# Two vision layers on one core: one stream of window pairs over all strips, queries in two buffers made a strip ahead, keys and values loaded in halves, one chain of square roots a strip

## What is computed

```
# layer 0: window attention with a halo, then a small network
x = x + proj(softmax(q k^T + relative position) v)   # 8x8 windows, 6 heads of 16,
                                                     # keys and values from the 12x12 around each window
x = x + quantised_mlp(layernorm(x))                  # 96 -> 384 -> 96, fp8 products
# layer 1: clustering, then a small network
f, v = conv1x1(norm(x))                              # folded into 4 quadrants, 4 heads
sim  = sigmoid(beta + alpha * cos(centres, f)); one centre wins for each point
x = x + proj(sum of the won centres' values)
x = x + quantised_mlp(layernorm(x))
```

## Time and profile before

| | us |
|---|---|
| median of 3 runs | 8823.7 (8789.32 to 8832.83) |
| the profiled execution, its own time | 8806.34 |
| its span, first to last instruction | 8804.6 |
| TensorE matmul busy | 6983.3 |
| TensorE weight loads busy (beside the matmuls) | 5559.6 |
| VectorE busy | 6471.8 |
| ScalarE busy | 4502.9 |
| GpSimd busy | 2616.0 |
| mean granted TensorE clock | 0.865 of 2.4 GHz |

### The profile page before, as it was taken

How to read it: one execution, slowest core, us unless ns; L and a number is a source line. 1 busy time by engine, 2 the same in 40 slices (tenths; PEclk the granted TensorE clock), 3 DMA queues, 4 the chain that set the end, 5 groups by cost and what they waited for, 6 DMA issues and landing times.

```text
span 8804.6 us, 408965 instructions
## 1 busy us (share of the span) xinstructions
PE 6983.3 (79%) x161908; PEld 5559.6 (63%) x161908; DVE 6471.8 (74%) x23705; ACT 4502.9 (51%) x8986; POOL 2616.0 (30%) x4382
## 2 busy tenths in 40 slices
PE   5888888877888888888888878888788878886555
PEld 4666666766666666666666666666666666664332
DVE  3666667667787778777787877777777878786566
ACT  2444444444555555555555555555555555554455
POOL 2333333232333232322323232322323233332112
PEclk7888888888998889888898988989898989898765
DMA  3333333333343433333333333434333333332211
GB/s 82 70 69 69 70 67 71 69 78 76 82 86 81 85 76 82 85 82 81 79 88 80 86 79 80 84 83 85 77 82 80 84 82 83 83 83 65 66 55 53
DMA packets 819501, 681.29 MB, mean 77 GB/s; under 512 B 656745, under 2 KB 690345, under 8 KB 817695
## 3 DMA queue, kind: packets, MB, share of 16 engines
q1 hardware_dynamic: 817918, 657.52, 34.0%
HBM read 350.43 MB, written 227.25 MB: 66 GB/s over the span
## 4 chain that ended last, share of the span: by engine, by line
PE 61%; DVE 15%; issue 13%; ACT 9%; DMA 1%; ACTq 1%; SPq 0%; POOL 0%; DVEq 0%; POOLq 0%
PE scores_x L718 11%; PE bank L695 8%; PE flipped L742 6%; DVE maxes L1562 4%; PE bank L698 4%; PE pv L769 3%; PE bank L678 3%; DVE shifted L1570 3%; PE bank L962 2%; PE bank L662 2%; PE flipped L989 2%; PE pv L763 2%; PE misc L796 2%; PE bank L671 2%; ACT probs L1239 2%
## 5 line engine op out<-in xcount | busy, mean ns | idle before, releaser
L1992 POOL TENSOR_SCALAR x_new<-x_new,mv_x,rs_x 120x96 f32<-120x96 f32 x1170 | 844.5, 734 | 4281.4 <-DVE rs_x L1468 4281.4
L1562 DVE TENSOR_REDUCE maxes<-scores_x 128x6 f32<-128x864 f32 x1024 | 1078.1, 1053 | 837.3 <-PE scores_x L718 831.0
L718 PE MATMUL scores_x<-keys,queries 64*64 64x144 f32 x24576 | 1114.8, 316 | 361.7 <-DVE shifted L1570 274.9
L698 PE MATMUL bank<-xr,wq 97*32 97x64 f32 x24576 | 1071.0, 253 | 216.1 <-issue 215.6
L695 PE MATMUL bank<-xt,wq 97*32 97x64 f32 x24576 | 1065.2, 253 | 222.5 <-issue 210.2
L718 PEld LDWEIGHTS scores_x<-keys,queries 64*64 64x64 f32 x24576 | 818.2, 146 | 560.8 <-issue 523.7
L695 PEld LDWEIGHTS bank<-xt,wq 97*32 97x32 f32 x24576 | 935.2, 132 | 339.9 <-issue 251.8
L698 PEld LDWEIGHTS bank<-xr,wq 97*32 97x32 f32 x24576 | 934.9, 132 | 262.6 <-issue 262.0
L1570 DVE TENSOR_TENSOR shifted<-scores_x,maxes 128x768 f32<-128x768 f32 x1024 | 970.4, 948 | 0.0
L1202 ACT ACTIVATE queries<-bank 128x512 f32<-128x512 f32 x768 | 456.0, 594 | 963.8 <-PE bank L698 961.2
L742 PE MATMUL flipped<-ident,shifted 128*128 128x128 f32 x6144 | 914.2, 288 | 0.6 <-ACT probs L1236 0.4
(11 more groups left out here) (194 smaller groups left out, 14423.0 us busy)
## 6 DMA issues: line engine op xcount, KB each, us to landing
vmain<-v_kept SPq DMA_DIRECT2D x384, 204.0 KB, 4.7
keys<-kst SPq DMA_DIRECT2D x768, 101.2 KB
v_kept<-v_new SPq DMA_DIRECT2D x128, 430.3 KB
x_new<-x_dram SPq DMA_DIRECT2D x130, 409.2 KB, 3.9
xn_kept<-xn SPq DMA_DIRECT2D x128, 388.0 KB, 3.7
later<-xn_kept SPq DMA_DIRECT2D x128, 388.0 KB, 3.3
x_tok<-tok_dram SPq DMA_DIRECT2D x128, 384.0 KB, 3.4
x_kept<-x SPq DMA_DIRECT2D x128, 384.0 KB, 4.4
```

What stands on the lines that cost most here:

```text
L698: last = mm(dst[64 * e + 32:64 * e + 64, :, j, :], wq[0:PROW, 2 * WS + j, 2 * g + e, :], xr[0:PROW, p, j, :, :], start=True, stop=True, sk ...
L718: last = mm(score[e][64 * j:64 * j + 64, g * NKEY:(g + 1) * NKEY], queries[64 * e:64 * e + 64, g, w, :], keys[64 * e:64 * e + 64, g, :, WS ...
L1562: V.tensor_reduce(maxes[:, p % 2, :, :], sc, AX.X, ALU.max).then_inc(max_ready.sem, 1)
L1992: last = P.tensor_scalar(x_new[:, t, 0:C], x_new[:, t, 0:C], mv_x[:, t, 0:1], rs_x[0:XP, t:t + 1], ALU.subtract, ALU.mult)
```

## The change

- **One stream of pairs.** The tail is gone. In pair 7 of strip `n`, TensorE makes the scores of pair 0 of strip `n + 1`; the last `weigh` of a strip stands in pair 0 of the next one. The filler work of all stages is dealt out anew over the eight pairs of all engines: a function of strip `n` is now often called one strip later (`flip_heads(n - 1, 1)`, `mix(n - 1, ...)`, `output(n - 2, ...)`).
- **Queries a strip ahead.** `queries` has two buffers. The six groups of strip `n + 1` are made in pairs 2, 4, 5 and 6 of strip `n`. `x1` has two buffers too.
- **Loads in halves.** Keys are loaded in 2 x 6 transfers and values in 2 x 11. The first half waits for the middle of the strip before, the second for its end.
- **One chain of roots a strip.** `all_roots` in pair 4 makes the roots for x, the stream, both halves of the network, stage c and the feature lengths in one chain of 65 columns.
- The input strip is loaded three strips ahead instead of two. The queue of SyncE has another order.

```
-        queries = sb("queries", [128, NG, NW, 64])
+        queries = sb("queries", [128, 2, NG, NW, 64])
...
+            def load_values(m, column, h):
+                if h == 0:
+                    sp.wait_ge(v_saved, m * 16 + V_TOPS + 16)
+                        sp.wait_ge(pv_ready.sem, pv_ready.at(m - 1, 4))
+                else:
+                    sp.wait_ge(pv_ready.sem, pv_ready.at(m, 0))
...
+            def load_keys(n, h):
+                if h == 0:
+                    sp.wait_ge(k_stored.sem, k_stored.at(n, 3))
+                    sp.wait_ge(halo_k.sem, halo_k.at(n, 1))
+                        sp.wait_ge(s_ready.sem, s_ready.at(n - 1, 4))
+                else:
+                    sp.wait_ge(s_ready.sem, s_ready.at(n, 0))
...
# TensorE
+            def strip(n, par, on, edge_=None):
+                for p in range(TILES):
+                    if p + 1 < TILES:
+                        scores(n, p + 1, par)
+                    elif ahead:
+                        scores(n + 1, 0, 1 - par)
+                    if p == 3 and on.b:
+                        features(n, 0)
...
+                    flip(n, p, 0, on)
+                    flip(n, p, 1, on)
+                    if p > 0:
+                        weigh(n, p - 1, on.bp)
+                    else:
+                            gather(n - 1, 1 - par)
+                            pool(n - 3)
+                            weigh(n - 1, TILES - 1)
+                    if p == 0:
+                            output(n - 2, 0)
+                            output(n - 2, 1)
+                            for u in range(2):
+                                pe.wait_ge(mixed.sem, mixed.at(n - 1, u + 1))
+                                flip_zc(n, u)
+                            make_keys(n + 1, 0, on)
+                            make_keys(n + 1, 1, on)
+                    if p in (1, 2) and on.c3:
+                        hidden_c(n, 2 * p - 2)
+                        hidden_c(n, 2 * p - 1)
+                    if p == 1:
+                            make_keys(n + 1, 2)
+                            make_values(n + 1, 0)
+                            make_values(n + 1, 1)
+                            flip_heads(n - 1, 1)
+                            edge(edge_[0], n, edge_[1], edge_[2], on)
+                    if p == 2:
+                            project(n - 1, 1)
+                            make_queries(n + 1, 0, on)
+                            make_queries(n + 1, 1, on)
+                    if p == 3:
+                            features(n, 1)
+                            hidden_c(n, 4)
+                            hidden_c(n, 5)
+                            flip_features(n + 1, 0, 1 - par)
+                    if p == 4:
+                            make_queries(n + 1, 2, on)
+                            flip_features(n + 1, 1, 1 - par)
+                            output_c(n, 0)
+                            output_c(n, 1)
+                            flip_sims(n)
+                    if p == 5:
+                            make_queries(n + 1, 3, on)
+                            hidden(n - 1, 0)
+                            hidden(n - 1, 1)
+                        flip_heads(n, 0, b1)
+                            make_queries(n + 1, 4, on)
...
# VectorE, behind the subtraction of pair p
+                    if p == 0:
+                            hidden(n - 2, 4)
+                            hidden(n - 2, 5)
+                            mix(n - 1, 0, 1 - par, work)
+                            mix(n - 1, 1, 1 - par, work)
+                            stats_c(n, 1 - par)
+                    if p == 1:
+                            normalise(n - 1, 1, slot if on.b3 else None, n - 3, n - 1 if on.bp else None)
+                            edge(edge_[0], n, edge_[1], edge_[2])
+                            output(n - 2, par)
+                            next_stats(n - 2)
...
+                    if p == 3:
+                            residual(n - 1, 1, 1 - par)
+                            ffn_stats(n - 1, 1, 1 - par)
+                            compare(n, 0)
+                            compare(n, 1)
+                            squares_sum(n, 0)
+                            squares_sum(n, 1)
+                    if p == 4:
+                        all_roots(n, 0, ROOTS, ...)
+                            cosine(n, n)
+                            ffn_apply(n - 1, 0, 1 - par, n)
+                    if p == 5:
+                        normalise(n, 0)
+                            ffn_apply(n - 1, 1, 1 - par, n)
+                            best_of(n, 0)
```

More of the change, by code:

```diff
@@ L605, in _ @@
                 first = max((j - 1) * COLUMN, LAG_C + 2)
-                with sp.Fori(0, (j * COLUMN - 2 - first) // 2) as s:
+                last = j * COLUMN - 2 if j < STARTS else N - 4
+                with sp.Fori(0, (last - first) // 2) as s:
                     for par in range(2):
@@ new lines, in project @@
+            def project(n, b, again=True):
+                pe.wait_ge(heads_t_ready.sem, heads_t_ready.at(n, b + 1))
+                if b == 0 and again:
+                    pe.wait_ge(zt_ready.sem, zt_ready.at(n - 1, 2))
+                pe.sem_inc(gate, 1)
+                for j in range(4):
+                    last = mm(misc[:, j * C:(j + 1) * C], heads_t[0:PROW, j * 128:(j + 1) * 128],
+                              wp[0:PROW, :], start=True, stop=True)
+                last.then_inc(proj_ready.sem, 1)
@@ L1140, in _ @@
                     n = STRIPS * r + 2 + k
-                    if n < N:
-                        strip(n, k, stage(n))
-                    else:
-                        drain(n, k, stage(n))
+                    drain(n, k, stage(n))
             for n in range(N + LAG_C, N + LAG_C + 2):
@@ L1402, in drain, with strips @@
                     for i in range(2 * NK):
-                        hidden_c(n, i)
+                        hidden_c(n + 1, i)
                         if i >= 1:
-                            quantise_c(n, i - 1)
-                    quantise_c(n, 2 * NK - 1)
+                            quantise_c(n + 1, i - 1)
+                    quantise_c(n + 1, 2 * NK - 1)
+            def strips(first, last, on):
+                with act.Fori(0, (last - first) // 2) as s:
+                    for par in range(2):
+                        strip(2 * s + (first + par), on, par)
             setup()
```

1407 lines of the change are left out of this document (710 added, 697 removed).

## The result

The changed kernel takes 8101.3 us (median of 4 runs, 8097.7 to 8113.1) against 8806.5 of the kernel before, run beside it: a ratio of 0.921, with a 95% interval of 0.916 to 0.925. Predicted were 8030 us with a range of 7650 to 8450. The profiled execution took 8113.1 us, its span is 8111.4, and the mean granted clock rose from 0.865 to 0.905.

A forecast was written before the change was run, and what follows sets the result against it. TensorE and VectorE, nearly equally loaded, wait for each other; a full strip was VectorE's 49.9 us plus TensorE's excesses, 58.0 with clock and edges. Savings of 526 + 126 + 125 = 777 us from 8806 gave 8030 us, range 7650 to 8450.

The forecast's parts named there:

- The tail and the one stream: Strip end, where no pair runs and two engines take turns: one stream of pairs can remove these waits; start and drain unchanged.
- Both start a block at about the same time.: Block p runs from subtraction p to p + 1; TensorE and VectorE start together, so it takes the longer one's time.
- block 2: From subtraction 2 to 3: TensorE's work with two query groups (2.8 us) takes 7.0 us with waits, 1.3 over VectorE.
- the chain of block 3: From subtraction 3 to 4: scores, features, square, `compare`, sum, maxima and subtraction in a row, 8.5 us, 2.9 over VectorE.
- Block 0 and `load_xc`: From subtraction 0 to 1: TensorE takes 7.3 us, 1.5 over VectorE, hiding the mix's 1.5 us wait for `load_xc`.
- its last part: Signs: even maxima distances, VectorE's busy time some 370 us less; wrong if `mix` waits several microseconds or non-3 pairs exceed 7.5.
- Halves of the loads: SyncE's queue: doubled transfers take 28.2 us instead of 14.1 a strip, but cost nothing while SyncE has slack.
- Rival 3: SyncE's queue becomes the bound: issues over 1.2 us each make the stream run at 66 us a strip, 9100 us; chance 0.06.
- The single chain of roots: VectorE: two of three root chains go, the 65-column one costs 0.23 us an instruction; 3.6 us a strip saved.
- my bounds: TensorE's clock in a full strip: cost between nothing and 5.5 us of 57; 0.3 us was taken.
- TensorE's 46.3 us: Strips of layer 0 alone: TensorE's work at the clock granted before bounds them; with 1.7 us of waits, 48 us.
- block 5: From subtraction 5 to 6: TensorE's work of 2.5 + 2.8 + 1.4 us given as 6.6 us, 0.6 over VectorE.

The follow-up runs named there:

- short_query_1: The changed kernel with seven eighths of the products of query group 1 (pair 2) left out on TensorE: 7944.9 us, ratio 0.903 to the kernel before.
- late_compare: The changed kernel with copy and sum of squares of the features' second half moved from VectorE's pair 3 to pair 4: 7855.0 us, ratio 0.892.
- xc_early: The changed kernel with SyncE issuing `load_xc` directly behind `store_out`, ahead of second keys and input strip: 7951.7 us, ratio 0.903 to the kernel before.
- whole_loads: The changed kernel with keys in 6 and values in 11 whole transfers, issued where the second halves stood: 9546.6 us, ratio 1.085 to the kernel before.
- split_roots: The changed kernel with a separate root chain for the feature lengths, directly behind the chain for the rest: 8197.9 us, ratio 0.934 to the kernel before.
- the last three kernels: The changed kernel with late second-half features, early `load_xc`, 10-strip ScalarE loop: 7688.5 us; plus `features(n, 0)` in pair 2: 7672.9; plus second copy/sum before `hidden_c`: 7663.8.
- the longer loop: The changed kernel with ScalarE's loop over full strips holding 10 strips an iteration instead of 2: 8053.4 us, ratio 0.917 to the kernel before.

## Why the prediction was right, and where not

**The tail and the one stream.** Right. The waits of maxima for scores are gone (831 to 112 us in all), the strips run through, start and drain did not move.

**"Both start a block at about the same time."** This step failed in blocks 2 and 3. TensorE's filler work of pair p delays scores p + 2, not scores p + 1, so it meets VectorE's work of the next block. I priced the two query groups in block 2 (7.0 us; it measured 5.6) and let the chain of block 3 begin at the subtraction (8.5; it measured 11.0). Together 16.6 us against 15.5. The chain itself was priced well: from scores 4 at 4167.6 to the end of the sum at 4173.9 it takes 6.3 us, where I had 6.3 without the maxima and subtraction; over the strips 36 to 123 its mean is 6.7. The 2.9 us ahead of it in that strip, 2.1 in the mean, are TensorE's lateness: short_query_1 shortens the block by 1.6 us by taking 1.6 us out of pair 2's query groups. And late_compare shows that 246 us of the wait can be won by order alone.

**Block 0 and `load_xc`.** The wait came as foretold in place and, with 199 us over 90 strips or 2.2 us each, in size (0 to 3, taken 1.5). What failed is "which block 0 hides": without it the time falls by 1.6 us for each of the 94 full strips (150 us). By the order of the code `flip_zc` on TensorE waits for the mix, so the wait delays both engines. And the load was later than priced: it went out some 12.4 us into block 6 at the median and not 11, and landed after 4.4 us at the median of the full strips and not 3.0, with the transfer of 409 KB ahead, which I had named and not priced. The prediction also said in its last part that the mix should wait little or not at all, and that a block other than 3 over 7.5 us would speak against it; block 0 took 8.2. I did not have ScalarE's gap at all: 48 us.

**Halves of the loads.** Right: SyncE issues six half keys in 4.8 us where six whole ones took 5.76, and does not set the pace of the strips. Its order still counts: these 4.8 us stand ahead of `load_xc` in the queue, and xc_early won 150 us by passing them. The rule of the Trainium skill that spoke against it ("DMA: Bandwidth & Descriptors", Rules for kernel authors: coalesce small transfers) would have made the time longer here: with whole transfers it is 9547 us. What counts here is when a transfer may start: a whole one goes out only when the strip before has done with the whole buffer. It also lands later (a whole transfer of values 4.9 us after its issue in whole_loads, a half 2.5 in the changed kernel), and no run parts the two. Rival 3, SyncE as the bound, is out.

**The single chain of roots.** Its length was right, 0.23 us an instruction at 65 columns. Its worth was not: I let all 3.6 us count, 1.8 for each chain removed. split_roots gives 97 us, 0.9 us for each of 110 strips, for one of them, out of 1.55 us that the block itself lost. In this place a microsecond on VectorE was worth a little over half; the other removed chain was not tested. VectorE's busy time fell by 317 us, not by the 370 of the prediction.

**Clock.** Lay between my bounds, but I used it only on one side. For layer-0 strips I took TensorE's 46.3 us at the clock granted before, 0.84. It is granted 0.98 now, and the same work takes 630.65/16 = 39.4 us. That is 6.9 us less work at the higher clock, and I read it as the main reason why these strips take 44.6 us and not 48. The waits beside it were under-priced: 5.2 us (44.6 - 39.4) where I took 1.7. A share of the gain is that query groups, no longer six in a row, have fewer gaps without a releaser: 197 us for L734 and L737 against 426 for L695 and L698 before. No run tells the two apart.

**Size.** The two query groups of pair 2 take 2.0 us where the trace shows no gap in them, but 2.8 us at the median, just what I took; the difference is gaps and clock. So the lateness of block 3 is not a matter of their price. One sum of the prediction is off by 0.1: block 5 adds up to 6.7 us, not 6.6. In all, the full strips lost 180 us against the forecast, and the others won 96.

**What stays open.** How much of the 346 us of the full strips is owed to the clock alone; what whole keys alone would cost; and what bounds blocks 3 and 4 in the last three kernels.

## What to carry to other kernels

In a software pipeline of in-order engines, follow each piece of filler work to the instruction that it really delays: on an engine that hands over first, it is the handover after the next. Price a removed microsecond by which engine leads in that block, and look for what the gain turns into one block later. Gaps for which the list of waits names nothing can be set beside the packets on the queues that load instructions. When the tail of a strip is taken away, look for everything that it used to hide: a late load, a loop's jump, a first wait.

## What was not expected of the hardware

- The jump back of ScalarE's loop costs 3.8 us (163.0 us, 43 times), and 3.5 in the longer loop (24.4 us, 7 times). In each of these gaps the trace has packets of instructions, as shown above. The kernel before loops over one strip at a time and has no such gap in its list; whether because its loop is half as long or because ScalarE rested in the tail, no run tells. The Trainium skill ("Advanced Engine Details and Errata", Control Flow Timing) gives about 0.1 us for a compare-and-branch. The gap of this trace is over thirty times that, so a jump back can cost far more than its branch.
- TensorE shows gaps of up to 2.0 us without a releaser in rows of small query products, 146 times in L734. In block 3 one of 1.14 us lies on the chain that ended last. Set beside the DMA packets of the trace, these gaps are no accident: each of the 198 of over 0.4 us (L734 and L737 together) ends 2.2 to 3.2 us after the start of the last 16 KB packet on queue 8, which the page lists as "instruction" as well, and each of the 219 of the kernel before 2.2 to 3.6 us after one. Of all query products only a third start 2.0 to 3.5 us behind such a packet. So I read them as TensorE waiting for its instructions; no run changes the loading by itself.
- A load of 384 KB (`load_xc`) lands 4.4 us after its issue at the median of the full strips, where a load of 409 KB is issued 0.85 us earlier. In the drain steps of the same kernel, where none is issued ahead, it lands after 3.0 us, and so it did in the full strips of the kernel before. In the strip shown the mix went on 5.2 us after the issue.
